# An attention stage with four PSUM banks for its scores instead of three, and three single banks for the maxima instead of two pairs

## The chip, the cores and the metric

One Trainium2 chip, one of its cores. The metric is the device time of the whole kernel in microseconds; less is better. The kernel before takes 2076.58 us (median of three runs, 2074.81 to 2076.8).

## The reference, cut to what matters

A layer on x of shape (2, 2048, 128) in fp32: half a mixture-of-experts block, attention, and half a mixture-of-experts block again. The change touches the attention only:

```
x = x + 0.5 * ffn(layernorm(x))
x = x + attn(layernorm(x))
x = x + 0.5 * ffn(layernorm(x))

# attn: 2 batches x 16 heads of dimension 8, sequence 2048
q, k, v = x @ wq.T, x @ wk.T, x @ wv.T       # per head; q and k with rms_norm and rope; q / sqrt(8)
scores = einsum('bqhd,bkhd->bhqk', q, k)
attn   = softmax(scores.astype(float32), axis=-1)
out    = einsum('bhqk,bkhd->bqhd', attn, v).reshape(b, s, 128) @ wo.T
```

## The kernel before

The program runs phase after phase: loads, norm, routing and experts, norm, q/k/v, attention, output, norm, routing and experts. The attention phase handles 32 heads (BH) one after another. For each head it needs two passes over all 2048 x 2048 scores.

- **The maxima.** For 16 groups of 128 queries and 4 chunks of 512 keys (64 matmuls of 512 columns, `maxima`, L1178) the scores are made with the queries on the partitions. VectorE reduces them over the keys (`reduce`, L1260): two banks at a time, 1024 columns, into `mx`, and once per head `mx` into `neg`, the negated maximum of each query (L1274). GpSimd splits this into three bf16 parts, TensorE turns them (`turn_maxima`, L1191, called T here), ScalarE copies them out (`keep_maxima`, L1146) and a DMA places them as three more rows of q.
- **The scores.** For 16 groups g of 128 keys and 4 chunks c of 512 queries the scores are made again with the keys on the partitions and the maximum subtracted by the three rows (`scores`, L1196, for the next head's first group `pe_next`, L1235). ScalarE takes the exp of each bank of 512 columns (L1135) into `at_prob`, and four matmuls of 32 output columns weigh the values with them (`weigh`, L1206), side by side in the array, into one accumulating bank O.

On TensorE the two are interleaved. In `turn`, step g issues for each chunk c a score matmul (called S0 to S3) on the array's lower rows and a maxima matmul (M0 to M3) on its upper rows, and after the four the weigh matmuls W of group g - 1. The maxima run ahead of the scores: step g up to LAG = 9 belongs to the next head's groups 7 to 15, step g above 9 to groups 0 to 6 of the head after the next. So turns 0 to 29 have maxima in every step, turn 30 in its first nine and turn 31 none. In front of the first turn stand 92 maxima matmuls alone (64 of head 0, 28 of head 1).

The eight banks of PSUM are split into a ring S of three banks for the scores, a ring M of two pairs for the maxima, and O. All order is written out by hand with semaphores that count. A score matmul with running number n waits until the exp n - 3 is done (`free`; T and its copy count as one entry in this ring). The first matmul of a pair of maxima waits until the reduce of the pair two before is done; a reduce waits for the second matmul of its pair. W waits for the four exps of its group, and the first W of a head also until ScalarE has copied the last head's sums out of O (`keep_sums`, L1140). TensorE takes its instructions in order, so what stands behind a waiting one waits too.

Of the kernel before, what the change touches and what calls it, by code (L numbers as in the profile page):

```python
# [16 lines left out]
ACT = mybir.ActivationFunctionType  # L17
AX = mybir.AxisListType

P = 128  # L20
# [4 lines left out]
BLK = 512  # L25
# [14 lines left out]
KT = SEQ // P  # L40
LN_EPS, RMS_EPS = 1e-5, 1e-6
BUFS = 3
PROBS = 4
# [6 lines left out]
KR = len(PAIRS) * HD  # L50
MR = 3
MROW = KR
KS = KR + MR
HALF = P // 2
# [932 lines left out]
def attention_phase(nc, sem, kept, ps, v, identb, q, k, vals, q_rows, k_rows, qk_loaded, qk_stored,  # L987
# [8 lines left out]

    CHUNKS = SEQ // BLK
    STEPS = KT * CHUNKS
    PAIRS_OF_HEAD = STEPS // 2
    ENTRIES = STEPS + 1  # L1000
    AHEAD, LAG = 2, 9
    TURNS = BH - AHEAD
    SRING = 3
    MRING = 2
    VSTEPS = 4
    TURN_MAXIMA = LAG + 3
    assert TURNS % BUFS == 0 and BUFS * ENTRIES % SRING == 0 and PAIRS_OF_HEAD % MRING == 0
    max_scored = sem("at_max_scored")
    max_reduced = sem("at_max_reduced")
    max_found = sem("at_max_found")  # L1010
# [4 lines left out]
    exped = sem("at_exped")  # L1015
# [4 lines left out]
    def turned_at(h):  # L1020

        return 0 if isinstance(h, int) and h == 0 else 1 + (h - 1) * ENTRIES + 4 * (TURN_MAXIMA + 1)

    def entry(h, g, c, last=False):

        return 1 + h * ENTRIES + g * CHUNKS + c + (1 if g > TURN_MAXIMA and not last else 0)

    def bank(i, g, c, last=False):

        return (1 + i * ENTRIES + g * CHUNKS + c + (1 if g > TURN_MAXIMA and not last else 0)) % SRING  # L1030

    def turned_bank(i):

        return (1 + (i - 1) * ENTRIES + 4 * (TURN_MAXIMA + 1)) % SRING

    with ExitStack() as tmp:
        mx = [kept(f"mx{i}", [P, KT, 2]) for i in range(BUFS)]
        neg = [kept(f"neg{i}", [P, KT]) for i in range(BUFS)]
        res = kept("res", [P, KT])
        zero = kept("zero", [P, KT])  # L1040
# [6 lines left out]
        inv = kept("inv", [P, BLK])  # L1047
        prob = tmp.enter_context(nc.sbuf_tensor("at_prob", [P, PROBS, CHUNKS, BLK], F32))
        block = tmp.enter_context(nc.Block())
        S, M, O = 0, SRING, SRING + 2 * MRING  # L1050

        @block.gpsimd
        def _(pool):
# [76 lines left out]
        @block.scalar  # L1130
        def _(act):
            def exps(h, i, g, last=False):
                for c in range(CHUNKS):
                    act.wait_ge(scored, entry(h, g, c, last) + 1)
                    act.activation(prob[:, g % PROBS, c, :], ps[:, S + bank(i, g, c, last), :], ACT.Exp).then_inc(exped, 1)  # L1135

            def keep_sums(h):
                act.wait_ge(weighed, (h + 1) * KT + PRIME)
                act.wait_ge(sums_stored, 16 * SUM_DMAS * h + PRIME)
                act.activation(sums[:], ps[:, O, :], ACT.Copy).then_inc(sums_kept, 1)  # L1140

            def keep_maxima(h, bank_at):
                act.wait_ge(scored, turned_at(h) + 1)
                if not (isinstance(h, int) and h == 0):
                    act.wait_ge(max_placed, 16 * h)
                act.activation(mrows[:], ps[0:MR * KT, S + bank_at, 0:P], ACT.Copy).then_inc(exped, 1)  # L1146

            def turn(h, i, last=False):
                for g in range(1, KT):
                    if not (isinstance(h, int) and h == 0 and g < PROBS):  # L1150

                        act.wait_ge(weighed, h * KT + max(g - PROBS, -1) + 1 + PRIME)
                    exps(h, i, g, last)
                    if g == TURN_MAXIMA and not last:
                        keep_maxima(h + 1, turned_bank(i + 1))
                if not last:
                    act.wait_ge(weighed, (h + 1) * KT - PROBS + 1 + PRIME)
                    exps(h + 1, i + 1, 0)
                keep_sums(h)

            prime(act, sums_kept)
            keep_maxima(0, 0)
            exps(0, 0, 0)
            for it in range(0, TURNS // BUFS):
                for i in range(BUFS):
                    turn(it * BUFS + i, i)
            turn(BH - 2, (BH - 2) % BUFS)
            turn(BH - 1, (BH - 1) % BUFS, last=True)

        @block.tensor  # L1170
        def _(pe):
            def maxima(h, i, j):

                n, c = h * PAIRS_OF_HEAD + j // 2, j % CHUNKS
                if j % 2 == 0 and not (isinstance(n, int) and n < MRING):
                    pe.wait_ge(max_reduced, n - MRING + 1)
                at = M + 2 * (j // 2 % MRING) + j % 2
                one = pe.matmul(ps[:, at, :], q[i][HALF:HALF + KR, (j // CHUNKS) * P:(j // CHUNKS + 1) * P],  # L1178
                                k[i][HALF:HALF + KR, c * BLK:(c + 1) * BLK], start=True, stop=True)
                if j % 2:  # L1180
                    one.then_inc(max_scored, 1)

            def free(n):

# [3 lines left out]
            def turn_maxima(h, i, bank_at):  # L1188
                free(turned_at(h))
                pe.wait_ge(max_split, (h + 1) * VSTEPS)  # L1190
                pe.matmul(ps[0:MR * KT, S + bank_at, 0:P], mparts[i][:].rearrange("p a t -> p (a t)"), identb[:],  # L1191
                          start=True, stop=True).then_inc(scored, 1)

            def scores(h, i, g, c, last=False):
                free(entry(h, g, c, last))
                pe.matmul(ps[:, S + bank(i, g, c, last), :], k[i][0:KS, g * P:(g + 1) * P],  # L1196
                          q[i][0:KS, c * BLK:(c + 1) * BLK], start=True, stop=True).then_inc(scored, 1)

            def weigh(h, i, g, last=False):
# [10 lines left out]
            def turn(h, i, loads=None, last=False):  # L1210


                nxt, far = (i + 1) % BUFS, (i + AHEAD) % BUFS
                for g in range(1, KT + 1):
                    if g == LAG + 1 and loads is not None:
                        pe.wait_ge(qk_loaded[far], 16 * LOAD_DMAS * loads)
                    if g == KT and not last:
                        pe.wait_ge(max_placed, 16 * (h + 2))
                    for c in range(CHUNKS):
                        if g < KT:  # L1220
                            scores(h, i, g, c, last)
                        elif not last:
                            pe_next(h, nxt, c, i)
                        if g <= LAG and not last:
                            maxima(h + 1, nxt, (KT - LAG + g - 1) * CHUNKS + c)
                        elif g > LAG and loads is not None:
                            maxima(h + AHEAD, far, (g - LAG - 1) * CHUNKS + c)
                    if g == TURN_MAXIMA and not last:
                        turn_maxima(h + 1, nxt, turned_bank(i + 1))
                    weigh(h, i, g - 1, last)  # L1230

            def pe_next(h, nxt, c, i):

                free(entry(h + 1, 0, c))
                pe.matmul(ps[:, S + bank(i + 1, 0, c), :], k[nxt][0:KS, 0:P],  # L1235
                          q[nxt][0:KS, c * BLK:(c + 1) * BLK], start=True, stop=True).then_inc(scored, 1)

            prime(pe, weighed)
# [15 lines left out]
        @block.vector  # L1254
        def _(dve):
            def reduce(h, i, j):

                dve.wait_ge(max_scored, h * PAIRS_OF_HEAD + j + 1)
                at = M + 2 * (j % MRING)
                dve.tensor_reduce(mx[i][:, j // 2, j % 2:j % 2 + 1], ps[:, at:at + 2, :].rearrange("p a t -> p (a t)"),  # L1260
                                  AX.X, ALU.max).then_inc(max_reduced, 1)

            def turn(h, i, last=False):


                for j in range(2, PAIRS_OF_HEAD):
                    reduce(h, i, j)
                if not last:
                    for j in range(2):
                        reduce(h + 1, (i + 1) % BUFS, j)  # L1270
                dve.wait_ge(max_reduced, (h + 1) * PAIRS_OF_HEAD)
                if not (isinstance(h, int) and h < BUFS):
                    dve.wait_ge(max_split, (h - BUFS + 1) * VSTEPS)
                dve.tensor_reduce(neg[i][:], mx[i][:], AX.X, ALU.max, negate=True).then_inc(max_found, 1)  # L1274

            for j in range(2):
                reduce(0, 0, j)
            for h in range(BUFS):
                turn(h, h)
            for it in range(1, TURNS // BUFS):  # L1280
                for i in range(BUFS):
                    turn(it * BUFS + i, i)
            for h in range(TURNS, BH):
                turn(h, h % BUFS, last=(h == BH - 1))
            dve.wait_ge(o_loaded[0], 16 * (1 + BPS))
            dve.reciprocal(inv[0:ROWS_OF_BATCH, :], den[0:ROWS_OF_BATCH, :]).then_inc(inverted, 1)
# [123 lines left out]
```

## Time and profile before

| | |
|---|---|
| median of three runs | 2076.58 us (2074.81 to 2076.8) |
| profiled execution | 2074.9 us, span 2073.1 us |
| TensorE matmul busy | 1854.9 us (89%) |
| VectorE busy | 1523.3 us (73%) |
| ScalarE busy | 1297.5 us (63%) |
| GpSimd busy | 333.6 us (16%) |
| mean granted TensorE clock | 0.953 |
| maxima reduces (L1260) | 1024, 1206.5 us busy |
| exps (L1135) | 2048, 1057.1 us busy |

The span is the time from the first to the last instruction of one profiled execution. The attention's maxima begin at about 409 us and its last sums are copied at 1746.8 us. In a line of groups stand the program's line, the engine, the operation, what it writes and reads, how many there are, their busy time, the mean time of one in ns, and the idle time of the engine before them with what ended it. "PEld" is TensorE's weight load, which is recorded apart from the matmul. Busy times are unions, so two matmuls that run side by side on different rows of the array count once.

### The profile page before, as it was taken

The page shows a single profiled execution, that of the slowest core. Times are in us where ns is not written, and L with a number is a line of the kernel's source. Part 1 is how long each engine was busy: PE and PEld are TensorE (multiplying, and loading weights), DVE is VectorE, ACT ScalarE, POOL GpSimd, SP SyncE. Part 2 cuts the span into 40 slices and gives each one's busy share as a digit, 9 for nine tenths or more (in the row PEclk, how much of TensorE's full clock was granted, in tenths as well). Part 3 has the DMA queues.
Part 4 walks back from the last instruction along what each step waited for, and adds up shares of the span by engine and source line. Part 5 has one row for each costly group of instructions (what it writes and reads, how often), then busy time and mean ns, then how long its engine had stood idle before and what let it go on. Part 6 is the DMA issues. An engine that isn't in the chain of part 4 may idle for free. (4 is left out here: it accounts for less than half of the span.)

```text
span 2073.1 us, 28446 instructions
## 1 busy us (share of the span) xinstructions
PE 1854.9 (89%) x10619; PEld 700.9 (34%) x10619; DVE 1523.3 (73%) x1691; ACT 1297.5 (63%) x2497; POOL 333.6 (16%) x394
## 2 busy tenths in 40 slices
PE   4699996579999999999999999999999998679999
PEld 3466664412222222222222222222222222456665
DVE  6333336489999999999999999999999961633333
ACT  2222224507888888888888888888888885222222
POOL 2355550300000000000000000000000000035554
PEclk9899997858999999999999999999999998689999
DMA  4543310300100000000000010000000001057663
GB/s 107 107 128 110 113 49 16 124 29 2 34 18 18 32 21 18 26 27 18 21 32 18 18 33 19 18 29 23 18 22 30 18 3 49 0 120 131 116 118 62
DMA packets 65155, 98.23 MB, mean 47 GB/s; under 512 B 12013, under 2 KB 31026, under 8 KB 65018
## 3 DMA queue, kind: packets, MB, share of 16 engines
q1 hardware_dynamic: 60858, 94.32, 18.3%
q10 hardware_dynamic: 4160, 2.10, 0.4%
q8 instruction: 84, 1.38, 0.3%
q14 instruction: 53, 0.43, 0.1%
HBM read 84.94 MB, written 11.04 MB: 46 GB/s over the span
## 5 line engine op out<-in xcount | busy, mean ns | idle before, releaser
L1260 DVE TENSOR_REDUCE at_mx<-ps 128x1 f32<-128x1024 f32 x1024 | 1206.5, 1220 | 76.3 <-PE ps L1178 37.8
L1135 ACT ACTIVATE at_prob<-ps 128x512 f32<-128x512 f32 x2048 | 1057.1, 602 | 201.8 <-PE ps L1196 189.5
L1178 PE MATMUL ps<-k_head,q_head 48*128 48x512 bf16 x2048 | 711.8, 395 | 30.4 <-PEq L773 23.5
L1196 PE MATMUL ps<-q_head,k_head 51*128 51x512 bf16 x1924 | 581.7, 383 | 75.8 <-ACT at_prob L1135 34.0
L1206 PE MATMUL ps<-at_prob,vals 128*32 128x512 f32 x4096 | 546.4, 605 | 0.1
L682 DVE TENSOR_TENSOR e_hidden<-e_part,ps 128x512 f32<-128x512 f32 (+1 forms) x208 | 143.0, 688 | 323.6 <-POOL e_part L659 318.6
L1196 PEld LDWEIGHTS ps<-q_head,k_head 51*128 51x128 bf16 x1924 | 143.1, 94 | 687.4 <-ACT at_prob L1135 579.1
L633 ACT ACTIVATE e_silu<-ps 128x512 f32<-128x512 f32 (+1 forms) x208 | 124.4, 598 | 323.5 <-PE ps L591 323.4
L659 POOL TENSOR_TENSOR e_part<-e_silu,e_cw 128x512 f32<-128x512 f32 (+1 forms) x208 | 264.3, 1271 | 380.4 <-ACT e_silu L633 200.5
L1178 PEld LDWEIGHTS ps<-k_head,q_head 48*128 48x128 bf16 x2048 | 150.8, 94 | 205.9 <-DVE at_mx L1260 179.8
L599 PE MATMUL ps<-e_hidden,wdown 128*128 128x512 f32 (+1 forms) x416 | 214.9, 599 | 2.0 <-DVE e_hidden L682 2.0
L591 PE MATMUL ps<-xnT_hi,wgate_hi 128*128 128x512 f32 x208 | 148.6, 714 | 11.2 <-DVE e_hidden L682 8.0
L1064 POOL TENSOR_TENSOR at_mparts<-at_neg,at_zero 128x16 bf16<-128x16 f32 x32 | 7.0, 220 | 841.7 <-DVE at_neg L1274 841.7
L1206 PEld LDWEIGHTS ps<-at_prob,vals 128*32 128x32 f32 x4096 | 80.6, 108 | 112.2 <-issue 108.2
L599 PEld LDWEIGHTS ps<-e_hidden,wdown 128*128 128x128 f32 (+1 forms) x416 | 77.4, 189 | 25.5 <-DVE e_hidden L682 9.8
L591 PE MATMUL ps<-xnT_hi,wgate_lo 128*128 128x512 f32 x208 | 82.6, 397 | 0.0
L591 PE MATMUL ps<-xnT_lo,wgate_hi 128*128 128x512 f32 x208 | 81.6, 393 | 0.0
L591 PE MATMUL ps<-xnT_hi,wup_hi 128*128 128x512 f32 x192 | 76.3, 398 | 0.0
L591 PE MATMUL ps<-xnT_hi,wup_lo 128*128 128x512 f32 x192 | 75.9, 395 | 0.0
L591 PE MATMUL ps<-xnT_lo,wup_hi 128*128 128x512 f32 x192 | 75.1, 391 | 0.0
L1056 POOL COPY vals<-v 128x128 f32<-128x128 f32 x32 | 9.1, 289 | 387.8 <-PE ps L1206 387.8
L591 PEld LDWEIGHTS ps<-xnT_hi,wgate_hi 128*128 128x128 f32 x208 | 39.4, 189 | 72.6 <-issue 50.0
(171 smaller groups left out, 926.0 us busy)
## 6 DMA issues: line engine op xcount, KB each, us to landing
e_cw<-comb_rows SPq DMA_DIRECT2D x80, 256.0 KB, 4.4
e_cw<-comb_rows SPq DMA_DIRECT2D x32, 224.0 KB, 6.1
e_cw<-comb_rows SPq DMA_DIRECT2D x32, 192.0 KB, 5.1
q_head<-q_rows SPq DMA_DIRECT2D x64, 96.0 KB
k_head<-k_rows SPq DMA_DIRECT2D x64, 96.0 KB
e_cw<-comb_rows SPq DMA_DIRECT2D x32, 160.0 KB, 4.6
e_cw<-comb_rows SPq DMA_DIRECT2D x48, 96.0 KB, 3.8
e_cw<-comb_rows SPq DMA_DIRECT2D x32, 128.0 KB, 6.3
```

Of the source, the lines that this page charges most:

```text
L591: last = pe.matmul(ps[:, bank + i, :], w[wp][:, cols], xnT[xp][:, tokens], start=(m == 0), stop=(m == len(PASSES) - 1))
L599: pe.matmul(ps[:, Y, :], wdown[0:rows[c], c, :], hidden[0:rows[c], (par + c) % 2, :], start=(c == 0), stop=(c == CH - 1)).then_inc(downed, 1)
L633: act.activation(silu[0:rows[c], i, :], ps[0:rows[c], GATE + i, :], ACT.Silu).then_inc(silued, 1)
L659: pool.tensor_tensor(part[0:rows[c], i, :], silu[0:rows[c], i, :], cw[0:rows[c], c, :], ALU.mult).then_inc(weighted, 1)
L682: dve.tensor_tensor(hidden[0:rows[c], i, :], part[0:rows[c], i, :], up, ALU.mult).then_inc(hidden_ready, 1)
L1056: pool.tensor_copy(vals[i][:, :, 0:HD], head).then_inc(values_placed, 1)
L1064: pool.tensor_tensor(mparts[i][:, 0, :], neg[i][:], zero[:], ALU.add).then_inc(max_split, 1)
L1135: act.activation(prob[:, g % PROBS, c, :], ps[:, S + bank(i, g, c, last), :], ACT.Exp).then_inc(exped, 1)
L1178: one = pe.matmul(ps[:, at, :], q[i][HALF:HALF + KR, (j // CHUNKS) * P:(j // CHUNKS + 1) * P], k[i][HALF:HALF + KR, c * BLK:(c + 1) * BLK] ...
L1196: pe.matmul(ps[:, S + bank(i, g, c, last), :], k[i][0:KS, g * P:(g + 1) * P], q[i][0:KS, c * BLK:(c + 1) * BLK], start=True, stop=True).th ...
L1206: last = pe.matmul(ps[32 * c:32 * c + 32, O, :], vals[i][:, g, :], prob[:, g % PROBS, c, :], start=(g == 0), stop=(g == KT - 1), skip_grou ...
L1260: dve.tensor_reduce(mx[i][:, j // 2, j % 2:j % 2 + 1], ps[:, at:at + 2, :].rearrange("p a t -> p (a t)"), AX.X, ALU.max).then_inc(max_redu ...
```

## The change

The score ring gets four banks. The maxima ring gets three single banks; each maxima matmul now signals and waits by itself, and each reduce reads one bank of 512 columns. `mx` holds four numbers per group instead of two. Bank numbers are counted over all heads.

```diff
-    SRING = 3
-    MRING = 2
+    SRING = 4
+    MRING = 3
...
-        mx = [kept(f"mx{i}", [P, KT, 2]) for i in range(BUFS)]
+        mx = [kept(f"mx{i}", [P, KT, CHUNKS]) for i in range(BUFS)]
...
-        S, M, O = 0, SRING, SRING + 2 * MRING
+        S, M, O = 0, SRING, SRING + MRING
...
             def maxima(h, i, j):
 
-                n, c = h * PAIRS_OF_HEAD + j // 2, j % CHUNKS
-                if j % 2 == 0 and not (isinstance(n, int) and n < MRING):
+                n, c = h * STEPS + j, j % CHUNKS
+                if n >= MRING:
                     pe.wait_ge(max_reduced, n - MRING + 1)
-                at = M + 2 * (j // 2 % MRING) + j % 2
-                one = pe.matmul(ps[:, at, :], q[i][HALF:HALF + KR, (j // CHUNKS) * P:(j // CHUNKS + 1) * P],
-                                k[i][HALF:HALF + KR, c * BLK:(c + 1) * BLK], start=True, stop=True)
-                if j % 2:
-                    one.then_inc(max_scored, 1)
+                pe.matmul(ps[:, M + n % MRING, :], q[i][HALF:HALF + KR, (j // CHUNKS) * P:(j // CHUNKS + 1) * P],
+                          k[i][HALF:HALF + KR, c * BLK:(c + 1) * BLK], start=True, stop=True).then_inc(max_scored, 1)
...
             def reduce(h, i, j):
 
-                dve.wait_ge(max_scored, h * PAIRS_OF_HEAD + j + 1)
-                at = M + 2 * (j % MRING)
-                dve.tensor_reduce(mx[i][:, j // 2, j % 2:j % 2 + 1], ps[:, at:at + 2, :].rearrange("p a t -> p (a t)"),
+                n = h * STEPS + j
+                dve.wait_ge(max_scored, n + 1)
+                dve.tensor_reduce(mx[i][:, j // CHUNKS, j % CHUNKS:j % CHUNKS + 1], ps[:, M + n % MRING, :],
                                   AX.X, ALU.max).then_inc(max_reduced, 1)
...
-                for j in range(2, PAIRS_OF_HEAD):
+                for j in range(4, STEPS):
                     reduce(h, i, j)
                 if not last:
-                    for j in range(2):
+                    for j in range(4):
                         reduce(h + 1, (i + 1) % BUFS, j)
-                dve.wait_ge(max_reduced, (h + 1) * PAIRS_OF_HEAD)
+                dve.wait_ge(max_reduced, (h + 1) * STEPS)
```

On TensorE one step of the steady part read so before, from S0 to the weigh matmuls (k_head,q_head are the maxima, q_head,k_head the scores; in brackets the semaphores that an instruction waits on):

```order
L1196 MATMUL ps<-q_head,k_head 128x512 [waits at_exped]
L1178 MATMUL ps<-k_head,q_head 128x512 [waits at_max_reduced]
L1196 MATMUL ps<-q_head,k_head 128x512 [waits at_exped]
L1178 MATMUL ps<-k_head,q_head 128x512
L1196 MATMUL ps<-q_head,k_head 128x512 [waits at_exped]
L1178 MATMUL ps<-k_head,q_head 128x512 [waits at_max_reduced]
L1196 MATMUL ps<-q_head,k_head 128x512 [waits at_exped]
L1178 MATMUL ps<-k_head,q_head 128x512
L1206 MATMUL ps<-at_prob,vals 32x512 [waits at_exped]
```

And the same step on TensorE after the change, where the lines have moved up by three to five:

```order
L1191 MATMUL ps<-q_head,k_head 128x512 [waits at_exped]
L1175 MATMUL ps<-k_head,q_head 128x512 [waits at_max_reduced]
L1191 MATMUL ps<-q_head,k_head 128x512 [waits at_exped]
L1175 MATMUL ps<-k_head,q_head 128x512 [waits at_max_reduced]
L1191 MATMUL ps<-q_head,k_head 128x512 [waits at_exped]
L1175 MATMUL ps<-k_head,q_head 128x512 [waits at_max_reduced]
L1191 MATMUL ps<-q_head,k_head 128x512 [waits at_exped]
L1175 MATMUL ps<-k_head,q_head 128x512 [waits at_max_reduced]
L1201 MATMUL ps<-at_prob,vals 32x512 [waits at_exped]
```

The matmuls keep their order. The second and the fourth maxima matmul have a wait of their own now, and what the waits count differs: M3 waits for the reduce of M0 of its own step, and S3 for the exp of S3 of the step before. On VectorE the 34 reduces ahead of the first `at_neg` become 68, and the 32 of each later head 64.

## Rows read from the trace of the kernel before

**Rows 1.** Busy time by stretch; columns in the first line.

```profile
core 0: us, PE busy (x) PEld busy (x) DVE busy (x) ACT busy (x) POOL busy (x), PEclk, DMA share, GB/s
...
1000.00:1100.00 100.00, 94.21 (x652) 22.51 (x648) 95.37 (x84) 84.38 (x166) 3.20 (x14) 1.00 0.07 23
```

**Rows 2.** Groups by line in 500 to 1500 us.

```profile
L1260 DVE TENSOR_REDUCE at_mx<-ps 128x1 f32<-128x1024 f32 x806 | 949.8, 1220 | 49.4 <-PE ps L1178 17.8
L1135 ACT ACTIVATE at_prob<-ps 128x512 f32<-128x512 f32 x1610 | 831.2, 602 | 152.5 <-PE ps L1196 142.5 <-PE ps L1235 10.0
```

**Rows 3.** Who waited for whom, 500 to 1500 us: total, times, longest.

```profile
PEld ps L1196 <- ACT at_prob L1135: 445.7, 704, 0.8
...
PEld ps L1178 <- DVE at_mx L1260: 111.0, 373, 0.3
...
DVE at_mx L1260 <- PE ps L1178: 17.8, 54, 0.4
```

**Rows 4.** One step in order of time: start, duration, what.

```profile
1000.28 0.39 PE L1196 MATMUL ps<-q_head,k_head 51*128 51x512 bf16 x1
1000.28 0.39 PE L1178 MATMUL ps<-k_head,q_head 48*128 48x512 bf16 x1
...
1000.51 0.38 PE L1178 MATMUL ps<-k_head,q_head 48*128 48x512 bf16 x1
...
1000.76 2.07 ACT L1135 ACTIVATE at_prob<-ps 128x512 f32<-128x512 f32 x4 [0.39 <-PE ps L1196]
...
1000.91 0.39 PE L1178 MATMUL ps<-k_head,q_head 48*128 48x512 bf16 x1
...
1001.41 0.39 PE L1196 MATMUL ps<-q_head,k_head 51*128 51x512 bf16 x1
1001.42 0.39 PE L1178 MATMUL ps<-k_head,q_head 48*128 48x512 bf16 x1
...
1001.74 1.06 PE L1206 MATMUL ps<-at_prob,vals 128*32 128x512 f32 x8
...
1002.73 0.39 PE L1196 MATMUL ps<-q_head,k_head 51*128 51x512 bf16 x1
```

**Rows 5.** Single reduces of VectorE beside that step.

```profile
999.64 1.21 DVE L1260 TENSOR_REDUCE at_mx<-ps 128x1 f32<-128x1024 f32 x1
...
1000.95 1.23 DVE L1260 TENSOR_REDUCE at_mx<-ps 128x1 f32<-128x1024 f32 x1
...
1002.09 1.22 DVE L1260 TENSOR_REDUCE at_mx<-ps 128x1 f32<-128x1024 f32 x1
```

**Rows 6.** All at_neg reduces: shortest/median/longest ns, first and last start.

```profile
L1274 DVE TENSOR_REDUCE at_neg<-at_mx x32: 174/176/186, 460.0 to 1691.8; 128x16 f32<-128x32 f32 x32
```

**Rows 7.** Step with the turned maxima, in order of time.

```profile
702.97 0.39 PE L1196 MATMUL ps<-q_head,k_head 51*128 51x512 bf16 x1
...
703.46 0.24 PE L1191 MATMUL ps<-identb,at_mparts 128*48 128x128 bf16 x1
...
703.62 1.07 PE L1206 MATMUL ps<-at_prob,vals 128*32 128x512 f32 x8
```

**Rows 8.** Around a head's end, in order of time.

```profile
713.44 1.06 PE L1206 MATMUL ps<-at_prob,vals 128*32 128x512 f32 x8
...
714.57 0.60 ACT L1140 ACTIVATE at_sums<-ps 128x512 f32<-128x512 f32 x1
...
716.03 1.06 PE L1206 MATMUL ps<-at_prob,vals 128*32 128x512 f32 x8
```

**Rows 9.** Exps back to back in the first steps.

```profile
473.35 4.03 ACT L1135 ACTIVATE at_prob<-ps 128x512 f32<-128x512 f32 x8 [7.18 <-PE ps L1196]
```

**Rows 10.** A step without maxima, in order of time.

```profile
1743.06 0.82 PE L1196 MATMUL ps<-q_head,k_head 51*128 51x512 bf16 x3
...
1744.20 0.39 PE L1196 MATMUL ps<-q_head,k_head 51*128 51x512 bf16 x1 [0.32 <-ACT at_prob L1135]
...
1744.52 2.21 PE L1206 MATMUL ps<-at_prob,vals 128*32 128x512 f32 x16
```

**Rows 11.** VectorE's groups, forms kept apart.

```profile
L682 DVE TENSOR_TENSOR e_hidden<-e_part,ps 128x512 f32<-128x512 f32 x192 | 132.0, 688 | 298.7 <-POOL e_part L659 293.7 <-PE ps L599 5.0
...
L277 DVE BATCH_NORM_STATS2 stats<-x 128x6 f32<-128x128 f32 x32 | 6.6, 278 | 4.2 <-DMA x<-in_L_attn_x_dram 4.2
...
L508 DVE COPY combT<-ps 9x512 f32<-9x512 f32 x8 | 5.4, 679 | 8.1 <-PE ps L528 8.1
```

**Rows 12.** VectorE's reduces ahead of the first step.

```profile
424.76 35.33 DVE L1260 TENSOR_REDUCE at_mx<-ps 128x1 f32<-128x1024 f32 x30
```

More of the change, by code:

```diff
@@ L998, in attention_phase @@
     STEPS = KT * CHUNKS
-    PAIRS_OF_HEAD = STEPS // 2
     ENTRIES = STEPS + 1
@@ L1002, in attention_phase @@
     TURNS = BH - AHEAD
-    SRING = 3
-    MRING = 2
+    SRING = 4
+    MRING = 3
     VSTEPS = 4
     TURN_MAXIMA = LAG + 3
-    assert TURNS % BUFS == 0 and BUFS * ENTRIES % SRING == 0 and PAIRS_OF_HEAD % MRING == 0
     max_scored = sem("at_max_scored")
@@ L1026, in entry, with bank, turned_bank @@
         return 1 + h * ENTRIES + g * CHUNKS + c + (1 if g > TURN_MAXIMA and not last else 0)
[L1028 to L1034, printed above, removed]
+    def bank(h, g, c, last=False):
+        return entry(h, g, c, last) % SRING
+    def turned_bank(h):
+        return turned_at(h) % SRING
     with ExitStack() as tmp:
-        mx = [kept(f"mx{i}", [P, KT, 2]) for i in range(BUFS)]
+        mx = [kept(f"mx{i}", [P, KT, CHUNKS]) for i in range(BUFS)]
         neg = [kept(f"neg{i}", [P, KT]) for i in range(BUFS)]
@@ L1134, in exps @@
                     act.wait_ge(scored, entry(h, g, c, last) + 1)
-                    act.activation(prob[:, g % PROBS, c, :], ps[:, S + bank(i, g, c, last), :], ACT.Exp).then_inc(exped, 1)
+                    act.activation(prob[:, g % PROBS, c, :], ps[:, S + bank(h, g, c, last), :], ACT.Exp).then_inc(exped, 1)
             def keep_sums(h):
@@ L1154, in turn @@
                     if g == TURN_MAXIMA and not last:
-                        keep_maxima(h + 1, turned_bank(i + 1))
+                        keep_maxima(h + 1, turned_bank(h + 1))
                 if not last:
@@ L1195, in scores @@
                 free(entry(h, g, c, last))
-                pe.matmul(ps[:, S + bank(i, g, c, last), :], k[i][0:KS, g * P:(g + 1) * P],
+                pe.matmul(ps[:, S + bank(h, g, c, last), :], k[i][0:KS, g * P:(g + 1) * P],
                           q[i][0:KS, c * BLK:(c + 1) * BLK], start=True, stop=True).then_inc(scored, 1)
@@ L1228, in turn @@
                     if g == TURN_MAXIMA and not last:
-                        turn_maxima(h + 1, nxt, turned_bank(i + 1))
+                        turn_maxima(h + 1, nxt, turned_bank(h + 1))
                     weigh(h, i, g - 1, last)
@@ L1234, in pe_next @@
                 free(entry(h + 1, 0, c))
-                pe.matmul(ps[:, S + bank(i + 1, 0, c), :], k[nxt][0:KS, 0:P],
+                pe.matmul(ps[:, S + bank(h + 1, 0, c), :], k[nxt][0:KS, 0:P],
                           q[nxt][0:KS, c * BLK:(c + 1) * BLK], start=True, stop=True).then_inc(scored, 1)
@@ L1274, in turn @@
                 dve.tensor_reduce(neg[i][:], mx[i][:], AX.X, ALU.max, negate=True).then_inc(max_found, 1)
-            for j in range(2):
+            for j in range(4):
                 reduce(0, 0, j)
```

## The prediction

> **What bounds the kernel now.** I read the granted clock and the busy shares by stretch first, then the groups of instructions by line, then who waited for whom, and last the order of time inside single steps. The attention stage is the long middle. At full granted clock both TensorE (94%) and VectorE (95%) look full there, ScalarE is at 84% [rows 1]. So the shares don't say which of them sets the pace; the waits must.
>
> The groups give the costs per instruction: a reduce over two banks is recorded with 1220 ns, an exp with 602 ns [rows 2]. The waits say that the score matmuls wait mostly for exps (445.7 us over 704 waits), the maxima matmuls wait 111.0 us for reduces, and VectorE waits little for any of them [rows 3].
>
> One step (one g of `turn`: four scores S0 to S3, four maxima matmuls M0 to M3 beside them, the four weigh matmuls W) shows why [rows 4]. S0 starts at 1000.28. The exps start at 1000.76, 0.48 later. S3 needs the bank of S0, since there are three: it starts at 1001.41, which is the first exp's 0.60 and 0.05 more. W follows at 1001.74 (0.32), and the next S0 at 1002.73 (0.99). These five pieces close a loop: 0.48 + 0.60 + 0.05 + 0.32 + 0.99 = 2.45 us with the rounding. VectorE's two reduces of a step start at 999.64 and 1000.95, and the next step's first at 1002.09: the same 2.45 us, split 1.31 and 1.14 [rows 5]. 1.14 is the pitch of reduces back to back (each begins 0.09 before the record of the last one ends), so VectorE could do a step in 2.28 and waits 0.17. TensorE could too. **The ring of three score banks is the bound, with VectorE 7% behind it.**
>
> A head is 39.7 us, (1691.8 - 460.0) / 31 [rows 6], against 16 x 2.453 = 39.25. The rest is two extras: in the step with the turned maxima (T, L1191) S3 starts at 702.97, T at 703.46 and W at 703.62 [rows 7], so W is 0.65 after S3 instead of 0.32, +0.33. And where ScalarE copies the finished sums (L1140) before it goes on, W is 2.59 after the last W (713.44 to 716.03) instead of 2.45, +0.14 [rows 8].
>
> **The change, part by part.** (1) Four score banks. S3 now waits for the exp of S3 in the step before. That exp begins at about S0 + 0.48 + 3 x 0.49 = 1.95 of its step (0.49 is the pitch of exps, (4.03 - 0.60) / 7, [rows 9]) and has ended by 2.6, when the next S3 isn't due before 2.51 + 0.66 = 3.17 (in the tail 1.97 + 0.66 = 2.63, just behind it). The loop is cut, and ScalarE needs 1.96 a step. Without maxima, TensorE is then the bound. The steps without maxima in the tail are 2.45 now; S0 to S2 are three in 0.82 there [rows 10], so the third starts 0.44 after the first, S3 could start at 0.66, W at 0.98, the next S0 at 1.97. There are 22 such steps (turn 30 from g = 10, turn 31 up to g = 15): 22 x (1.98 - 2.45) = **-10.3 us**.
>
> (2) Single reduces. Instructions double (1024 to 2048 of this line) and each reads 512 columns. No row shows this form, so it has to be bounded. The fixed part of the pitch: 1.141 - 1024/0.96 ns = 1.141 - 1.067 = 0.074; the batch-norm statistics, back to back over 128 columns, give 6.6/32 = 0.206, less 0.133 = 0.073 [rows 11]. The two agree at eight times the size, so I take 0.533 + 0.075 = 0.608 for the pitch and 4 x 0.608 = 2.43 us of VectorE per step: 0.15 more than the 2.28 of now, but still under 2.45. The upper bound is no overlap at all, 0.69 each. In maxima-only work ahead of the first step, 92 maxima, VectorE is the bound: 30 reduces in 35.33 us now, 1.175 a pair [rows 12], then 1.216: 46 x 0.041 = **+1.9 us**.
>
> (3) Three maxima banks. M3 waits now for R0, the reduce of M0 in its own step; before, M2 and M3 waited for the last pair of the step before, and M0 for the first pair of it. Behind M3 stand W and the next M0 in TensorE's order, and the next R0 waits for that M0. So there is a new loop, R0, M3, W, M0, R0:
> - R0's own time. It starts after an idle moment, as the 1.225 of such reduces [rows 5]; less 0.533 that is 0.692. Other single-bank reads of PSUM: 0.688 and 0.679; a small reduce 0.176 - 0.033 = 0.143 fixed, so 0.676 [rows 6, 11]. Taken: 0.69, bounds 0.676 to 0.692.
> - from its end to the matmul that waited: 999.64 + 1.21 = 1000.85 to 1000.91, 0.06 [rows 4, 5].
> - M3 to W 0.32, W to the next S0 0.99, M0 at the same time as S0 to within 0.01, all [rows 4]. The 0.32 holds when the last matmul started alone too: in the tail S3 at 1744.20, W at 1744.52 [rows 10].
> - M0's own 0.39, and 0.06 to the reduce (M1 1000.51 + 0.38 = 1000.89, reduce 1000.95).
>
> Sum, unrounded pieces of those rows: 0.690 + 0.057 + 0.316 + 0.994 + 0.004 + 0.386 + 0.067 = **2.514 us**, which is over both VectorE's 2.43 and today's 2.453. There are 480 steps in turns 0 to 29 and 9 of turn 30, 489 x (2.514 - 2.453) = **+29.8 us**.
>
> (4) The extras. T waits for exp 0 now (ends at S0 + 1.14) and M3 starts at about S0 + 1.20, so T stands right behind M3. I know T to W, 0.16 [rows 7]; for M3 to T I have only M3 to W, 0.32, and at the least its 0.22 of streaming. T thus adds 0.06 to 0.16, I take 0.15 as both are a change of the array's shape: 30 x (0.15 - 0.33) = **-5.4 us**. The copy of the sums is over at about 3.25 after the start of a head's last step, the first W that needs it is due at 2.51 + 1.52 = 4.03: the 0.14 goes, 30 x 0.14 = **-4.2 us**. In the tail both stay about as they are. The one at_neg reduce per head (0.09 of pitch) fits in the 0.08 that VectorE waits. The wider `mx` adds 32 columns to it, 0.03 a head, 1 us in all if nothing hides it.
>
> **Sum:** 29.8 - 10.3 + 1.9 - 5.4 - 4.2 = +11.8, say +12 us on the profiled execution's 2074.9 (its span is 2073.1), so 2087. The median of the runs is 1.7 above the profiled one: 2088.5. The surplus is small against the loop: each 0.01 us in it is 4.9 us.
>
> **A rule weighed.** The statistics and the reduces begin before the last one's record has ended [rows 5, 11]. The Trainium skill, VectorE: DVE Perf Modes, section The DRAIN you can't avoid, says that the next operation doesn't start until the pipe is empty, but that one which isn't held starts earlier; by its first half a step would be 4 x 0.69 = 2.76. The trace bears out the second half so far. The same page, section on the TRN2 errata, gives 120 cycles plus the columns for a PSUM source, 0.658 us for one bank as an estimate by the page; the loop would then be 2.48.
>
> **Rivals.**
> A. *Faster: the turnover from M3 to W is hidden.* Of the 0.32 only 0.22 is streaming of 512 columns (S1 to S2 in the tail, 0.44 / 2). If W's weights get in while TensorE sits waiting for M3, the loop is 2.41 and VectorE's 2.43 takes over: 489 x -0.02 = -10, and with the other terms -18, -28 in all: 2049. It decides from a turnover under 0.24 (0.316 - 0.082). For it: TensorE is idle at that point now. Against: the tail's S3 also waited idle, and W still came 0.32 after it.
> B. *Each single reduce is shorter than the nearest rows say.* At 0.658 the loop is 2.48, +0.029 x 489 = +14, less 18: 2071 profiled, 2073 median. The point where the sum is nil is a loop of 2.49, R0 at 0.666, which is 0.010 under the lowest row.
> C. *Much slower: no overlap between single reduces.* 4 x 0.69 = 2.76, +0.307 x 489 = +150, prologue 46 x 0.205 = +9, extras and tail -24: about 2210. Against it: 1.14 and 0.206 above.
> D. *The bank count isn't felt*, the loop I draw hides in something: then VectorE's 2.43 decides as in A.
>
> **Numbers.** My forecast (2079 to 2100) 0.64, A and D 0.13, B 0.14, C 0.04, something between my loop and C (separate waits of M1 and M3 that cost TensorE, 2100 to 2150) 0.05. Within 0.2% (4 us, about what a measurement of this kernel can tell) is the upper part of B and the bottom of mine. Slower 0.70, same 0.12, faster 0.18. The range reaches into B and a loop of 2.55: 2064 to 2106; that of my forecast alone is 2079 to 2100.
>
> **What would show it.** In the changed kernel's steady step W should follow W at 2.51; the single reduce is 0.68 to 0.69, R0 comes after a wait of about 0.08, R1 to R3 at 0.61. TensorE should wait for VectorE at M3 (about 0.5 a step) and nearly nowhere for ScalarE. The steps without maxima should be 1.98, the step with T 0.15 longer than the others, the one after the sums no longer. A pitch of 0.69, a turnover of 0.22, or a step of 2.43 would each prove a rival; a granted clock below 1.0 in the stage would upset all of it.

## The result, and the profile after

The changed kernel takes 2089.86 us (median of four runs, 2088.61 to 2090.56) against 2076.02 us for the kernel before (2074.81 to 2076.8): a ratio of 1.0061, with a 95% interval of 1.0048 to 1.0075. It is slower by 14 us, where 12 were forecast (2088.5 us). The profiled span is 2087.3 us, 14.2 us more than before. The mean granted clock is 0.954 (0.953 before).

In the steady steps the busy shares of VectorE and TensorE now are 98% and 93% at full granted clock (before: [rows 1]). Busy time by stretch, then, for 500 to 1500 us, the groups of the reduces and the exps (their lines are now L1255 and L1133):

```profile
1000.00:1100.00 100.00, 93.28 (x637) 22.23 (x639) 98.31 (x161) 83.53 (x164) 2.62 (x11) 1.00 0.08 27
```

```profile
L1255 DVE TENSOR_REDUCE at_mx<-ps 128x1 f32<-128x512 f32 x1581 | 981.8, 683 | 17.8 <-PE ps L1175 5.1
L1133 ACT ACTIVATE at_prob<-ps 128x512 f32<-128x512 f32 x1580 | 815.5, 604 | 166.5 <-PE ps L1191 154.8 <-PE ps L1230 11.7
```

The share misleads again: VectorE is at 98% and is still not what sets the step, as the experiments below show. In the same 1000 us it completes 1581 single reduces, worth 790 pairs, where it completed 806 [rows 2]. Who waited for whom, 500 to 1500 us (total, times, longest):

```profile
PEld ps L1175 <- DVE at_mx L1255: 305.3, 754, 0.7
PEld ps L1191 <- ACT at_prob L1133: 269.0, 321, 0.8
...
PE ps L1175 <- DVE at_mx L1255: 68.1, 395, 0.2
...
DVE at_mx L1255 <- PE ps L1175: 5.1, 25, 0.2
```

The maxima matmuls' wait for reduces has grown from 111.0 to 305.3 us, the score matmuls' wait for exps has shrunk from 445.7 to 269.0 [rows 3]; and that rest is mostly time in which TensorE ran W anyway: the weight load behind W is recorded as idle for 0.84, and 0.84 x 321 is all of the 269.0. The loop itself is seen in one step, in order of time: M3, W, the next S0 and M0.

```profile
1002.47 0.39 PE L1175 MATMUL ps<-k_head,q_head 48*128 48x512 bf16 x1 [0.17 <-DVE at_mx L1255]
1002.78 1.07 PE L1201 MATMUL ps<-at_prob,vals 128*32 128x512 f32 x8
1003.78 0.39 PE L1191 MATMUL ps<-q_head,k_head 51*128 51x512 bf16 x1
1003.78 0.39 PE L1175 MATMUL ps<-k_head,q_head 48*128 48x512 bf16 x1
...
1005.30 1.07 PE L1201 MATMUL ps<-at_prob,vals 128*32 128x512 f32 x8
```

And VectorE's single reduces beside it, R0 (the one after the wait), R1 to R3, and the next R0:

```profile
1001.72 0.69 DVE L1255 TENSOR_REDUCE at_mx<-ps 128x1 f32<-128x512 f32 x1
...
1002.33 0.68 DVE L1255 TENSOR_REDUCE at_mx<-ps 128x1 f32<-128x512 f32 x1
...
1002.92 0.68 DVE L1255 TENSOR_REDUCE at_mx<-ps 128x1 f32<-128x512 f32 x1
...
1003.52 0.68 DVE L1255 TENSOR_REDUCE at_mx<-ps 128x1 f32<-128x512 f32 x1
...
1004.24 0.69 DVE L1255 TENSOR_REDUCE at_mx<-ps 128x1 f32<-128x512 f32 x1
```

R0 ends at 1002.41, M3 starts 0.06 later at 1002.47, W at 1002.78, S0 and M0 at 1003.78, the next R0 at 1004.24. From R0 to R0 that is 2.52 us, and from W to W too. R1 to R3 follow at 0.60; only in front of R0 does VectorE wait, 0.12 (1004.24 - 1003.52 - 0.60). Before, a step was 2.45 [rows 4, 5]. With T (L1186) in it, W comes 2.69 after the last W (990.01 to 992.70), and behind the copied sums 2.52 like any other:

```profile
990.01 1.07 PE L1201 MATMUL ps<-at_prob,vals 128*32 128x512 f32 x8
...
992.53 0.24 PE L1186 MATMUL ps<-identb,at_mparts 128*48 128x128 bf16 x1
...
992.70 1.06 PE L1201 MATMUL ps<-at_prob,vals 128*32 128x512 f32 x8
```

A step without maxima, in the tail, is 1.96 us, W to W (before: 2.45, [rows 10]):

```profile
1740.31 1.06 PE L1201 MATMUL ps<-at_prob,vals 128*32 128x512 f32 x8
1741.30 1.03 PE L1191 MATMUL ps<-q_head,k_head 51*128 51x512 bf16 x4
1742.27 1.07 PE L1201 MATMUL ps<-at_prob,vals 128*32 128x512 f32 x8
```

I also counted the distances from the start of one W to the start of the next over the whole phase. The 488 up to the end of the maxima have grown from 1213.6 to 1236.3 us (+22.6), and the last 23 have shrunk from 55.5 to 45.6 us (-9.9). The first W begins 1.2 us later, and 0.3 us is found behind the last. Together 14.2 us, the whole difference of the spans.

### The profile page after: what moved, and what is told of

Its sections match the earlier page's. It is cut to its first block and busy times, and to the rows that moved or that the text cites. A ratio compares the mean times of both kernels' runs of the same rounds, so it can differ in the third digit from the quotient of the medians.

```text
span 2087.3 us, 29470 instructions
## 1 busy us (share of the span) xinstructions
PE 1874.0 (90%) x10619; PEld 709.5 (34%) x10619; DVE 1585.6 (76%) x2715; ACT 1294.9 (62%) x2497; POOL 333.8 (16%) x394
## 5 line engine op out<-in xcount | busy, mean ns | idle before, releaser
L1255 DVE TENSOR_REDUCE at_mx<-ps 128x1 f32<-128x512 f32 x2048 | 1269.7, 683 | 36.9 <-PE ps L1175 21.2
L1133 ACT ACTIVATE at_prob<-ps 128x512 f32<-128x512 f32 x2048 | 1055.1, 604 | 214.9 <-PE ps L1191 200.9
L1175 PE MATMUL ps<-k_head,q_head 48*128 48x512 bf16 x2048 | 665.4, 395 | 107.8 <-DVE at_mx L1255 83.9
L1191 PE MATMUL ps<-q_head,k_head 51*128 51x512 bf16 x1924 | 499.7, 380 | 0.1
```

Source lines behind the costliest of these rows:

```text
L1133: act.activation(prob[:, g % PROBS, c, :], ps[:, S + bank(h, g, c, last), :], ACT.Exp).then_inc(exped, 1)
L1175: pe.matmul(ps[:, M + n % MRING, :], q[i][HALF:HALF + KR, (j // CHUNKS) * P:(j // CHUNKS + 1) * P], k[i][HALF:HALF + KR, c * BLK:(c + 1) * ...
L1191: pe.matmul(ps[:, S + bank(h, g, c, last), :], k[i][0:KS, g * P:(g + 1) * P], q[i][0:KS, c * BLK:(c + 1) * BLK], start=True, stop=True).th ...
L1255: dve.tensor_reduce(mx[i][:, j // CHUNKS, j % CHUNKS:j % CHUNKS + 1], ps[:, M + n % MRING, :], AX.X, ALU.max).then_inc(max_reduced, 1)
```

## The experiments

Each ratio is against the kernel before on the same chip. Its median was 2076.02 to 2077.82 us in the different groups of runs, so times from two groups can be compared to about 2 us.

**Three score banks, three single maxima banks.** It takes the score part of the change back and leaves the rest.

```diff
-    SRING = 4
+    SRING = 3
     MRING = 3
```

> The changed kernel with three score banks again and its three single maxima banks kept (one bank stands idle). My theory, that the loop R0, M3, W, M0, R0 over three maxima banks sets 2.52 us a step: the steps with maxima stay at 2.52, those without go back from 1.96 to 2.45 (22 x 0.49 = +11 us), the step with T waits for exp 1 again (T at S0 + 1.63, W 0.17 later, +0.11 a head) and the copied sums cost up to 0.18 a head. In all about 2104 to 2110 us. Rival, that the fourth score bank itself costs something in the steady steps: they fall to about 2.45 and the time is near 2080.

Measured: 2103.44 us, ratio 1.0128 (1.0113 to 1.0143), just under the expected range. The steady step stays at 2.52, here from W to W:

```profile
999.82 1.07 PE L1201 MATMUL ps<-at_prob,vals 128*32 128x512 f32 x8
...
1002.34 1.07 PE L1201 MATMUL ps<-at_prob,vals 128*32 128x512 f32 x8
```

In the tail it is 2.45 again. The extras are back too: 2.79 in the step with T and 2.59 after the sums. The fourth score bank is therefore worth 13.6 us (2103.44 - 2089.86), and what it is worth lies in the tail and in the extras, not in the steady step: up to the last W the two traces differ by 15.5 us, 9.9 in the tail and 5.8 in the 488 distances, and behind it this run was about 2 us shorter for no reason that the change gives. What the kernel gains there, the maxima ring takes away.

**Three score banks, four single maxima banks.** The maxima loop gets its fourth bank, and VectorE keeps its 2048 single reduces.

```diff
-    SRING = 4
-    MRING = 3
+    SRING = 3
+    MRING = 4
```

> Three score banks and four single maxima banks. My theory: with a fourth bank M3 waits for the last step's R3, the maxima loop is cut and the score loop of 2.45 us sets the pace, though VectorE has twice the reduces (4 x 0.598 = 2.39). Step 2.453, extras per head as before (0.33 and 0.14), about 2077 us, the same as the kernel before within 2 us. Rival, that the doubled reduces and their semaphores make the step long: 2.52 a step, and with the score loop in the tail 2104 to 2110 us.

Measured: 2078.13 us, ratio 1.0004 (0.9994 to 1.0014). One step in order of time, from one W to the next:

```profile
1000.30 1.06 PE L1201 MATMUL ps<-at_prob,vals 128*32 128x512 f32 x8
1001.30 0.39 PE L1191 MATMUL ps<-q_head,k_head 51*128 51x512 bf16 x1
...
1002.43 0.39 PE L1191 MATMUL ps<-q_head,k_head 51*128 51x512 bf16 x1 [0.31 <-ACT at_prob L1133]
1002.44 0.39 PE L1175 MATMUL ps<-k_head,q_head 48*128 48x512 bf16 x1
1002.75 1.06 PE L1201 MATMUL ps<-at_prob,vals 128*32 128x512 f32 x8
```

S3 waits for the exp, M3 comes at once behind it, and the step is 2.45. Twice the reduces cost nothing here. This run differs from the one above only in the fourth maxima bank, so the 2.52 comes from the maxima ring having three single banks and from nothing else.

**W behind M1 instead of M3.** Four score and three maxima banks as in the change.

```diff
+                        if c == 1:
+                            weigh(h, i, g - 1, last)
                     if g == TURN_MAXIMA and not last:
                         turn_maxima(h + 1, nxt, turned_bank(h + 1))
-                    weigh(h, i, g - 1, last)
```

> The changed kernel with the weigh matmuls W moved from behind M3 to behind M1. My theory: any maxima matmul just in front of W waits for the reduce of the one that stood just behind the last W, so the loop only changes its names (R2, M1, W, M2, R2) and stays 2.51 to 2.52; T no longer stands in it and may save 0.17 a head: 2084 to 2090 us. Rival, that the place of W behind M3 is what hurts: the step falls to VectorE's 2.40 and the time to about 2030 us.

Measured: 2152.39 us, ratio 1.0362 (1.0347 to 1.0378). Both expectations fall. The step is 2.56:

```profile
1000.60 1.07 PE L1201 MATMUL ps<-at_prob,vals 128*32 128x512 f32 x8
...
1001.60 0.39 PE L1191 MATMUL ps<-q_head,k_head 51*128 51x512 bf16 x1
...
1002.02 2.07 ACT L1133 ACTIVATE at_prob<-ps 128x512 f32<-128x512 f32 x4 [0.49 <-PE ps L1191]
...
1003.15 1.07 PE L1201 MATMUL ps<-at_prob,vals 128*32 128x512 f32 x8
```

I had overlooked that W of group g - 1 waits for the exp of S3 of that group, and S2 and S3 now stand behind the last W. That makes a new loop: W to S2 1.00, to its exp 0.42, the exp of S3 0.49 later and 0.61 long, then W 0.03 after its end: 2.55. It is longer than 2.52 and hides the maxima loop, so this run doesn't tell the two theories apart. The first W of a head waits for the copied sums besides, and comes 3.14 after the last. In the last turn the granted clock is 0.50 in addition (1.2 GHz, from 1768.8 us on), and a step 3.68. In 1755 to 1765, just before it fell, TensorE had been busy for 8.3 of 10 us (busy time by stretch, the clock third from the end):

```profile
1755.00:1765.00 10.00, 8.32 (x49) 1.92 (x49) 0.00 (x0) 8.15 (x18) 0.00 (x0) 1.00 0.01 1
1775.00:1785.00 10.00, 10.00 (x36) 1.74 (x34) 3.35 (x1) 6.20 (x12) 0.00 (x0) 0.50 0.00 0
```

Against the changed kernel the 488 distances are 31.3 us longer, and the last 23, where the clock fell, 29.5 us.

**W between S3 and M3.** This asks the same question without that fault: W stays behind S3, but M3 is behind W.

```diff
+                        if c == CHUNKS - 1:
+                            weigh(h, i, g - 1, last)
                         if g <= LAG and not last:
                             maxima(h + 1, nxt, (KT - LAG + g - 1) * CHUNKS + c)
...
-                    weigh(h, i, g - 1, last)
```

> The changed kernel with W between S3 and M3, so that no W waits for M3. W still comes after S3, and so no exp stands in a new loop. My theory: M2, which now stands in front of W, waits for R3 of the step before, and the M3 behind W feeds this R3: R3, M2, (S3), W, M3, R3 is as long as the old loop, and the step stays 2.51 to 2.53; T has no W behind it, up to -0.17 a head: 2083 to 2096 us. Rival, that M3's wait in front of W is what hurts, whatever stands behind W: the step falls to VectorE's 2.40, about 2030 us.

Measured: 2070.29 us, ratio 0.9968 (0.9955 to 0.998). The rival's 2.40 and 2030 us don't come; the loop does change names and stays. But it is 2.49, not 2.51 to 2.53, and the time is 13 us under the expected range. Here M2 and S3 go ahead of W, and M3 and S0 behind it:

```profile
1002.22 0.39 PE L1175 MATMUL ps<-k_head,q_head 48*128 48x512 bf16 x1 [0.30 <-DVE at_mx L1256]
1002.22 0.39 PE L1191 MATMUL ps<-q_head,k_head 51*128 51x512 bf16 x1
1002.53 1.07 PE L1201 MATMUL ps<-at_prob,vals 128*32 128x512 f32 x8
1003.53 0.39 PE L1175 MATMUL ps<-k_head,q_head 48*128 48x512 bf16 x1
1003.54 0.39 PE L1191 MATMUL ps<-q_head,k_head 51*128 51x512 bf16 x1
```

```profile
1001.47 0.69 DVE L1256 TENSOR_REDUCE at_mx<-ps 128x1 f32<-128x512 f32 x1
...
1003.96 0.69 DVE L1256 TENSOR_REDUCE at_mx<-ps 128x1 f32<-128x512 f32 x1
```

The reduce ends at 1002.16, M2 starts at 1002.22, W at 1002.53, M3 at 1003.53, at the same distances as in the changed kernel. The next reduce starts 0.42 to 0.43 after its matmul (1003.96 - 1003.53) instead of 0.46 (1004.24 - 1003.78). That alone makes the 0.03. It is 15 us over the 488 steps; the rest of the gain, 4 us, is T, which has no W behind it and adds 0.03 instead of 0.17.

**The maxima matmul first in each pair.** W stays behind both; only S and M of a pair change places.

```diff
                     for c in range(CHUNKS):
-                        if g < KT:
-                            scores(h, i, g, c, last)
-                        elif not last:
-                            pe_next(h, nxt, c, i)
                         if g <= LAG and not last:
                             maxima(h + 1, nxt, (KT - LAG + g - 1) * CHUNKS + c)
                         elif g > LAG and loads is not None:
                             maxima(h + AHEAD, far, (g - LAG - 1) * CHUNKS + c)
+                        if g < KT:
+                            scores(h, i, g, c, last)
+                        elif not last:
+                            pe_next(h, nxt, c, i)
```

> The changed kernel with the maxima matmul ahead of the score matmul in each pair, W behind both as before. In the run with W between S3 and M3 the loop's pieces were all the same but one: the reduce began 0.423 us after its matmul instead of 0.455. My reading: the matmul that is started first of a pair side by side is done earlier. Then the step is 2.49 here too, about 2074 us (489 x -0.031). Rival, that the 0.032 belonged to the place right behind W or to something else there: the step stays 2.52 and the time about 2090 us.

Measured: 2074.58 us, ratio 0.9984 (0.9975 to 0.9994), as my reading had it. W to W is 2.49 (1001.77 to 1004.26):

```profile
1001.77 1.06 PE L1201 MATMUL ps<-at_prob,vals 128*32 128x512 f32 x8
1002.77 0.39 PE L1175 MATMUL ps<-k_head,q_head 48*128 48x512 bf16 x1
1002.77 0.39 PE L1191 MATMUL ps<-q_head,k_head 51*128 51x512 bf16 x1
...
1003.29 1.58 ACT L1133 ACTIVATE at_prob<-ps 128x512 f32<-128x512 f32 x3 [0.32 <-PE ps L1191]
...
1004.26 0.64 PE L1201 MATMUL ps<-at_prob,vals 128*32 128x512 f32 x4
```

The same trace shows the other side of the exchange. The score matmul is now the second of its pair, and ScalarE's first exp starts 0.51 after it (1003.29 - 1002.77) instead of 0.48 [rows 4]. So what counts is the place in the pair, not which rows of the array a matmul uses.

The exchange of two matmuls takes back the whole loss of the change: its 2089.86 becomes 2074.58. The loop's length is what counts, down to 0.03 us of it.

**W in two halves, in the changed kernel.** The other test by length: W is cut into matmuls of 256 columns, one half behind M1, one behind M3. Only the first half of a head's first W starts the accumulation.

```diff
+                cols = slice(part * BLK // 2, (part + 1) * BLK // 2)
                 for c in range(CHUNKS):
-                    last = pe.matmul(ps[32 * c:32 * c + 32, O, :], vals[i][:, g, :], prob[:, g % PROBS, c, :],
-                                     start=(g == 0), stop=(g == KT - 1), skip_group_check=True)
-                last.then_inc(weighed, 1)
+                    done = pe.matmul(ps[32 * c:32 * c + 32, O, cols], vals[i][:, g, :], prob[:, g % PROBS, c, cols],
+                                     start=(g == 0 and part == 0), stop=(g == KT - 1), skip_group_check=True)
+                if part:
+                    done.then_inc(weighed, 1)
...
+                        if c == 1:
+                            weigh(h, i, g - 1, 0, last)
...
-                    weigh(h, i, g - 1, last)
+                    weigh(h, i, g - 1, 1, last)
```

> The changed kernel with W cut into two halves of 256 columns, one behind M1 and one behind M3. My theory: the loop contains only half of W, 0.69 + 0.06 + 0.32 + 0.57 + 0.46 = 2.10 us, so VectorE decides with 4 x 0.598 = 2.39 us a step, 489 x -0.12 = -59 us; TensorE needs about 2.2 (0.54 + 0.57 twice), so the 22 steps without maxima become slower than 1.96 by 0.26, +6 us. About 2030 to 2042 us. Rival, that something else than W in the loop holds the step at 2.52: about 2095 us. If the granted array time of the halves is more than I think (each over 0.65), the step is 2.45 or more.

Measured: 2032.02 us, ratio 0.9782 (0.9768 to 0.9797), 58 us less than the changed kernel. The group of the reduces, 500 to 1500 us, shows VectorE as the bound: 1667 reduces in 1000 us with 0.1 us idle ahead of them, 0.60 each, 2.40 a step.

```profile
L1260 DVE TENSOR_REDUCE at_mx<-ps 128x1 f32<-128x512 f32 x1667 | 999.1, 675 | 0.1
```

**W in two halves, three score and four single maxima banks.** The same edit with SRING = 3 and MRING = 4.

> Three score banks, four single maxima banks, and W in halves of 256 columns. My theory: with halves both loops are shorter than VectorE's four reduces, so how the seven banks are shared no longer matters, and only the number of reduces does: 2.39 a step, 2028 to 2038 us as with four and three banks (2032). Rival, that the pairs of banks or the split of the banks, not the doubled reduces, make the 59 us between the two kernels with halves: 1975 to 2000 us.

Measured: 2030.72 us, ratio 0.9775 (0.9761 to 0.979), the same as with four and three within what these runs can tell. Once no loop is longer than VectorE's work, the sharing of the banks is worth nothing.

**W in two halves, in the kernel before.** Here the reduces are over two banks again.

> The kernel before (three score banks, two pairs of maxima banks) with W cut into two halves of 256 columns, behind M1 and behind M3. My theory: the score loop holds only half of W, 0.48 + 0.60 + 0.05 + 0.32 + 0.57 = 2.02, TensorE needs 2.2 (1.10 to 1.11 a half step was measured where nothing else bound), so VectorE decides with two reduces of 1024 columns, 2.28 a step: 489 x -0.17 = -83 us and 22 x -0.24 = -5 in the tail, +0.2 to 0.3 for each head at T and at the sums (8 us at most): 1985 to 2000 us. It also shows what the doubled reduces cost where VectorE is the bound: 0.11 us a step against the changed kernel with the same cut (2032 us), 489 x 0.11 = 54 us. Rival, that one of the two pairs is filled too late: 2.39 a step or more, no better than 2032 us.

Measured: 1972.95 us, ratio 0.9498 (0.9483 to 0.9512), 12 us less than the range I gave and the fastest of all. Its group of reduces in 500 to 1500 us, and the busy times in 100 us of it:

```profile
L1265 DVE TENSOR_REDUCE at_mx<-ps 128x1 f32<-128x1024 f32 x879 | 998.9, 1210 | 2.2 <-PE ps L1178 0.3
```

```profile
1000.00:1100.00 100.00, 99.02 (x1063) 25.75 (x1059) 99.64 (x91) 95.29 (x181) 3.21 (x14) 1.00 0.06 21
```

879 reduces in 1000 us are 1.14 each, 2.28 a step, against 2.40 with single ones. Here the doubled number of reduces costs its price, 489 x 0.12 = 59 us, and 59 us lie between the two kernels (2032.02 - 1972.95). I had added up to 8 us for T and the sums. Instead, even the 0.47 a head (14 us) that they cost in the kernel before is gone: the 488 distances are 2.28 on the mean with them in it (1113.6 us, against 1213.6 before). The step with the sums is still 2.71 and two others 2.35 and 2.45, but most others are 2.21 to 2.26: TensorE catches up while VectorE goes on without a break.

## Why the prediction was right

**The new loop** was the step on which the sign hung. Forecast 2.514 us, measured 2.521: R0 0.69, 0.06 to M3, 0.31 to W, 1.00 to S0, 0.46 to the next R0. The 0.007 too little are 3.4 us over 489 steps. Most of it is W to the next S0, taken as 0.994; it is 0.998 to 0.999 in both traces. The run with four single maxima banks shows that having three is the cause, the two runs with another order show that the loop's length moves the time as it should, and the halves show that W belongs to it. The statement that VectorE would not be the bound at 98% is shown by the run with the maxima matmul first (2.49 with the same reduces).

**The cut score loop in the tail**: forecast 22 x (1.98 - 2.45) = -10.3, measured -9.9 over the last 23 distances. The step itself is 1.96; against that I left out 0.49 us at the very end, where the last W waits for exps that have fallen behind TensorE, and 0.34 at the last head's boundary, where two W distances of 2.22 and 2.19 took the place of one of 2.59.

**The single reduce**: duration 0.683 on the mean, 0.69 after a wait, as taken. The pitch is 0.598, not 0.608: the reduce after a wait is followed after 0.61, the others after 0.60. The forecast took its 0.074 from a reduce that followed a wait. This mattered little, since VectorE has 0.12 to spare in a step, and made the maxima-only work at the front dearer by 1.2 instead of 1.9 us.

**The extras**: T adds 0.17 (2.69 - 2.52), just over the upper bound of 0.16 and not the 0.15 taken; the 0.14 of the copied sums is gone, as worked out. Of the at_neg reduce I wrote that 0.09 fits in a wait of 0.08, which it doesn't; the wait is 0.12, and no step is longer for it.

**The sum**: steady part with the extras +20.2 forecast and +22.6 measured, tail -10.3 and -9.9, front +1.9 and +1.2, together +11.8 and +14.2 with 0.3 behind. The mechanism and each term stand; the loop was mis-sized by 0.007 us. The loop's 3.4 us too little are in part made up by 1.2 us that the forecast doesn't name. Four steps of the kernel before take 2.73, since ScalarE begins its exps 0.28 later in them than in the others; why is open. In the changed kernel ScalarE is late by the same 0.28 in the same four steps, but they take 2.52: with four score banks there is room for it. The first step is 0.1 shorter besides.

**The rivals.** A, a hidden turnover from M3 to W: it is 0.31 in the new kernel although TensorE waits for M3, so it doesn't hide. B, a shorter single reduce: R0 is 0.69. The estimate of 0.658 from the Trainium skill (VectorE: DVE Perf Modes, section The TRN2 errata) is too short here. C, no overlap between reduces: R1 follows R0 after 0.61 with 0.69 on record. That goes against what the Trainium skill says first in that page's section The DRAIN you can't avoid, that the next operation waits for the empty pipe, and is allowed by its exception for an operation that isn't held. D, a bank count that isn't felt: three against four maxima banks is 25 us (2103.44 and 2078.13).

One statement of mine was too general: that the place of W doesn't matter for the loop. It holds for the maxima banks, but moving W makes other loops, and with W behind M1 the step ran into one of exps.

## What to carry to other kernels

With rings of buffers between engines, write down for every resource the loop from its last consumer through whatever stands in order in front of the next producer. The longest of these loops is the step, unless one engine's own work is longer still, and an engine at 98% can still be waiting on a loop. Moving a bank from one ring to the other only changes which loop is longest. What shortens them all is to cut the long block that stands in every loop (here W, 1.0 us, in two halves: 3% of the changed kernel, 5% of the one before), and then the number of instructions on the engine that becomes the bound decides.

## What the runs showed of the hardware

Of two matmuls side by side on different rows of the array, started 0.004 us apart, the first gives its result to the waiting engine earlier. On the maxima's rows it is 0.423 us from the start to the reduce for the first of a pair and 0.455 for the second. On the scores' rows it is 0.483 to the first exp of a step for the first and 0.514 for the second. The 0.031 is the same on either rows, so the order makes it. Exchanging the two saved 0.031 us in each step, because the reduces stand in the loop and the exps don't. Why an order of 0.004 makes 0.031 stays open.

A single reduce that follows a wait is recorded with 0.691 us and the next starts 0.608 after it; one in a chain takes 0.68 and is followed after 0.598.
